# An expert stage whose token rows arrive in 256-byte runs and are turned by VectorE, with all first matrices resident in SBUF

## What is computed

```python
h = layernorm(x)
logits = h @ Wg + bg                                  # 8 experts
vals, idx = top_k(logits, 2); w = softmax(vals)       # each token goes to 2 experts
hid = relu(h @ W1[e] + b1[e])                         # W1: 8 x 256 x 512
eo  = hid @ W2[e] + b2[e]                             # W2: 8 x 512 x 256
mixed = sum(eo[idx] * w)
x = x + layernorm_affine(mixed + h, gamma, beta)
```

## Time and profile before

| | us |
|---|---|
| median of 3 runs | 2424.22 (2422.47 to 2425.36) |
| span of the profiled execution, from its first to its last instruction | 2425.2 |

### The profile page before, as it was taken

One profiled execution on the slowest core, in us unless ns is written; L12 is line 12 of the kernel. 1 busy time (PEld: TensorE's weight loads), 2 busy tenths in 40 slices (PEclk: granted clock), 3 DMA queues, 4 the chain that ended last, 5 costly groups with the idle time before them and its releaser, 6 DMA issues. The chain is left out here.

```text
span 2425.2 us, 47399 instructions
## 1 busy us (share of the span) xinstructions
PE 2186.3 (90%) x13721; PEld 1766.3 (73%) x13722; DVE 2038.4 (84%) x3037; ACT 1506.5 (62%) x3292; POOL 1827.8 (75%) x1093
## 2 busy tenths in 40 slices
PE   8889899998989898998989898999787999999980
PEld 5667677677777666777777776767676999999970
DVE  5999999999999999999999999999974555555558
ACT  6687877878786877878787878877741111111106
POOL 3888989889898989889888989898962434444447
PEclk9999999999999999999999999999987999999995
DMA  5041322314041323324041413223137998999978
GB/s 172 7 134 54 131 75 102 124 52 164 21 158 48 131 69 114 106 70 153 32 156 34 144 49 135 80 96 116 62 123 199 226 228 229 229 230 229 229 166 277
DMA packets 186791, 312.50 MB, mean 129 GB/s; under 512 B 18851, under 2 KB 118083, under 8 KB 186500
## 3 DMA queue, kind: packets, MB, share of 16 engines
q1 hardware_dynamic: 140932, 258.53, 33.4%
q0 software_dynamic: 25584, 34.62, 7.5%
q10 hardware_dynamic: 20112, 17.32, 2.2%
HBM read 247.09 MB, written 63.32 MB: 128 GB/s over the span
## 5 line engine op out<-in xcount | busy, mean ns | idle before, releaser
L855 POOL TENSOR_TENSOR dbu<-drive_u,b_rows 128x1024 f32<-128x1024 f32 x384 | 904.3, 2363 | 87.7 <-DVE ps_a L660 35.1
L1159 ACT ACTIVATE ps_a<-delta,a_neg 128x512 f32<-128x512 f32 x768 | 517.2, 685 | 136.9 <-DVE ss L660 120.2
L872 POOL TENSOR_TENSOR wp<-ss,rows_c 128x1024 f32<-128x1024 f32 x192 | 453.6, 2363 | 37.6 <-DVE ss L660 36.9
L1766 POOL DMA_INDIRECT acc_scratch<-ow,idx x135 | 211.2, 1564 | 309.2 <-issue 102.4
L672 DVE TENSOR_TENSOR wd<-ps_a,rows_c 128x1024 f32<-128x1024 f32 x320 | 383.3, 1198 | 0.0
L1437 PEld LDWEIGHTS ps_y<-ident,wd 128*128 128x128 f32 x2560 | 299.4, 143 | 98.7 <-issue 70.5
L1437 PE MATMUL ps_y<-ident,wd 128*128 128x128 f32 x2560 | 337.3, 277 | 12.4 <-DVE wd L672 12.4
L1804 ACT COPY e_meta<-xt 128x2 f32<-128x2 f32 x135 | 25.9, 192 | 439.0 <-PE e_ps_x L1877 294.4
L1464 PEld LDWEIGHTS ps_a<-dg,duT 128*128 128x128 f32 x2048 | 248.6, 196 | 60.6 <-issue 58.1
L1464 PE MATMUL ps_a<-dg,duT 128*128 128x128 f32 x2048 | 259.0, 281 | 31.6 <-ACT carry L1166 28.6
L1688 DVE TENSOR_SCALAR e_hT<-e_ps_h,b_turned 128x128 f32<-128x128 f32 x540 | 152.1, 344 | 144.7 <-PE e_ps_h L1886 125.2
(11 more groups left out here) (200 smaller groups left out, 3653.8 us busy)
## 6 DMA issues: line engine op xcount, KB each, us to landing
b_rows<-in_L_ffn_W_dram SPq DMA_DIRECT2D x135, 512.0 KB
rows_c<-b_scratch SPq DMA_DIRECT2D x128, 512.0 KB, 4.9
b_rows<-b_scratch SPq DMA_DIRECT2D x96, 512.0 KB, 4.1
xt<-xs_scratch SPq DMA_DIRECT2D x135, 129.0 KB
xb<-in_L_attn_x_dram SPq DMA_DIRECT2D x16, 512.0 KB, 4.0
hx<-in_L_attn_x_dram SPq DMA_DIRECT2D x16, 512.0 KB, 6.3
x_scratch<-hx SPq DMA_DIRECT2D x16, 512.0 KB, 2.9
acc_scratch<-stage SPq DMA_DIRECT2D x16, 512.0 KB, 2.9
```

The source lines that it names most:

```text
L855: pool.tensor_tensor(dbu[:, k % NBU], du[:, g % 2, :].unsqueeze(1).broadcast_to([P, 2, CH]), bb[:, row:row + 2, :], ALU.mult).then_inc(dbu ...
L872: pool.tensor_tensor(wp[:, s % 2], ss[:, s % 2], cc[:, rows, :], ALU.mult).then_inc(wp_done, 1)
L1159: act.activation(dst, dl[:, g, :], ACT.Exp, scale=a_neg[:, g, n:n + 1]).then_inc(exp_done, 1)
L1766: pool.indirect_dma_start(out=acc_dram, out_offset=bass.IndirectOffsetOnAxis(ap=idx[:, old, :], axis=0), in_=ow[:, old, :], in_offset=None ...
```

## The change

The rows of a tile now load with four DMAs, one for each quarter of the 256 columns, each into 32 partitions. Partition 32 i + b of a slot holds, for each j of 4, columns 64 i to 64 i + 63 of row 32 j + b: 128 runs of 256 bytes in each DMA. A fifth DMA loads weight and row number of 128 rows, 8 bytes each, into `xm`. VectorE turns the slot in one instruction of 32x32 blocks into `xT`, in which partition p then has columns 2p and 2p + 1. TensorE no longer turns anything, and `e_ps_x` is only kept as space for the last stage (`e_ps_n`). W1 is stored in the matching order, rows 2p and 2p + 1 in partition p.

All 8 first matrices (4 MB) stay in SBUF, in `w1_all`, one tensor that holds the Mamba block's `win` and `b_rows` before. Seven DMAs load them while the last chunk ends. Per tile there is no W1 load and no second value load on SyncE; ScalarE copies the tile's W1 (128x1024) inside SBUF to one of two buffers `w1s` instead.

```diff
+            sync.wait_ge(proj_full, full("z", 3, NC - 1))
+            sync.dma_start(*w1_parts[0]).then_inc(w1_in, 16)
             for h in range(2):
+                for m in ((0, 1, 3, 4), (6, 7))[h]:
+                    sync.wait_ge(dbu_done, products(t, m))
+                    sync.dma_start(*w1_parts[brow(m) + 1]).then_inc(w1_in, 16)
                 sync.wait_ge(wd_done, ND * t + (3, 5)[h])
                 sync.wait_ge(wp_done, 3 * t + (2, 3)[h])
                 sync.dma_start(*experts[h]).then_inc(w_ready, 16)
...
-            sync.wait_ge(tabs, 11)
-            for j in range(W1_EARLY):
-                e = sync.value_load(tabi[0:1, 1, j:j + 1], min_val=0, max_val=E - 1)
-                sync.dma_start(w1[:, j], w1_t[:, bass.ds(e, 1)].rearrange("p e k f -> p (e k) f")
-                               ).then_inc(w1_in[j], 16)
...
-                wait_apart(sync, passed, [(x_copied, 1, t, 1 - RING)])
-                sync.dma_start(xt[:, slot, :], xs_dram[bass.ds(off, P), :]).then_inc(t_in[slot], 16)
-
-            def load_weights(t, slot):
-                e = sync.value_load(tabi[0:1, 1, bass.ds(t, 1)], min_val=0, max_val=E - 1)
-                wait_apart(sync, passed, [(h_full, 1, t, 1 - RING)])
-                sync.dma_start(w1[:, slot], w1_t[:, bass.ds(e, 1)].rearrange("p e k f -> p (e k) f")
-                               ).then_inc(w1_in[slot], 16)
+                wait_apart(sync, passed, [(x_turned, 1, t, 1 - RING), (meta_copied, 1, t, 1 - RING)])
+                rows = xs_dram[bass.ds(off, P), :].rearrange("(j b) d -> b j d", b=BLK)
+                for i in range(QB):
+                    sync.dma_start(xt[i * BLK:(i + 1) * BLK, slot], rows[:, :, i * D // QB:(i + 1) * D // QB]
+                                   ).then_inc(t_in[slot], 16)
+                with nc.allow_non_contiguous_dma(reason="a weight and a row number for each row"):
+                    sync.dma_start(xm[:, slot], xs_dram[bass.ds(off, P), D:]).then_inc(t_in[slot], 16)
...
+                if real(s):
+                    wait_slot(dve, t_in[slot], s, RING, slot, per=16 * PARTS)
+                    wait(dve, h_full, 1, s, -1)
+                    dve.transpose(xT[:, par], xt[:, slot].rearrange("p j (a k) -> p j k a", k=KD)).then_inc(x_turned, 1)
                 if real(s - 1):
...
+            act.wait_ge(tabs, 11)
+            act.wait_ge(w1_in, 16 * (E - 1))
...
                 if real(s):
-                    wait(act, x_turned, 1, s, 1)
+                    e = act.value_load(tabi[0:1, 1, bass.ds(s, 1)], min_val=0, max_val=E - 1)
+                    wait(act, h_full, 1, s, -1)
+                    act.copy(w1s[:, par].rearrange("p k f -> p (k f)"), w1[:, bass.ds(e * (KD * F), KD * F)]
+                             ).then_inc(w1_set, 1)
+                    wait_slot(act, t_in[slot], s, RING, slot, per=16 * PARTS)
                     wait(act, o_weighed, 1, s, 1 - RING)
-                    act.copy(meta[:, slot, :], xt[:, slot, D:])
-                    wait(act, h_full, 1, s, -1)
-                    act.copy(xT[:, par].rearrange("p k n -> p (k n)"), ps_x[:, par, 0:KD * P]).then_inc(x_copied, 1)
+                    act.copy(meta[:, slot, :], xm[:, slot]).then_inc(meta_copied, 1)
...
-                if real(s):
-                    wait_slot(pe, t_in[slot], s, RING, slot)
-                    wait(pe, x_copied, 1, s, -1)
-                    for k in range(KD):
-                        ins = pe.transpose(ps_x[:, par, k * P:(k + 1) * P], xt[:, slot, k * P:(k + 1) * P], ident[:])
-                    ins.then_inc(x_turned, 1)
                 if real(s - 1):
                     t = s - 1
-                    wait(pe, x_copied, 1, t, 1)
-                    wait_slot(pe, w1_in[(slot + 3) % RING], t, RING, (slot + 3) % RING)
+                    wait(pe, x_turned, 1, t, 1)
+                    wait(pe, w1_set, 1, t, 1)
                     wait(pe, h_done, 1, t, -1)
                     for j in range(KF):
                         for k in range(KD):
-                            ins = pe.matmul(ps_h[:, 1 - par, j, :], w1[:, (slot + 3) % RING, k, j * P:(j + 1) * P],
-                                            xT[:, 1 - par, k, :], start=(k == 0), stop=(k == KD - 1))
+                            ins = pe.matmul(ps_h[:, 1 - par, j, :], w1s[:, 1 - par, k, j * P:(j + 1) * P],
+                                            xT[:, 1 - par, :, k, :], start=(k == 0), stop=(k == KD - 1))
```

More of the change, by code:

```diff
@@ L16 @@
 U32 = mybir.dt.uint32
-W1_RING = 4
-W1_EARLY = 1
+RING = 4
+BLK = 32
 def wait(eng, sem, per, c, k):
@@ L83, in mamba_moe_kernel @@
                             W2[half].rearrange("e (k p) d -> p e k d", p=P)))
-        b_rows = ctx.enter_context(nc.sbuf_tensor("b_rows", [P, (N - 4) * CH], F32))
+        w1_all = ctx.enter_context(nc.sbuf_tensor("w1_all", [P, KD * 2 * DI + (N - 4) * CH], F32))
+        win_flat = w1_all[:, 0:KD * 2 * DI]
+        b_rows = w1_all[:, KD * 2 * DI:]
         delta = ctx.enter_context(nc.sbuf_tensor("delta", [P, G * CH], F32))
         drive_u = ctx.enter_context(nc.sbuf_tensor("drive_u", [P, 2 * CH], F32))
-        assert E * D == G * CH and W1_RING * KD * F <= (N - 4) * CH
-        w1 = b_rows[:, 0:W1_RING * KD * F].rearrange("p (r k f) -> p r k f", r=W1_RING, k=KD)
-        w1_t = W1.rearrange("e (k p) f -> p e k f", p=P)
+        assert E * D == G * CH and E * KD * F == KD * 2 * DI + (N - 4) * CH and 2 * KD * F == KD * 2 * DI
+        w1_t = W1.rearrange("e (p k) f -> p e (k f)", k=KD)
+        w1_e = w1_all[:].rearrange("p (e n) -> p e n", e=E)
+        w1_parts = [(w1_e[:, 0:2], w1_t[:, 0:2])] + [(w1_e[:, e], w1_t[:, e]) for e in range(2, E)]
         b2b, gm, bt = delta[:], drive_u[:, 0:D], drive_u[:, D:2 * D]
@@ L93, in mamba_moe_kernel @@
         small_in = ctx.enter_context(nc.semaphore("rows_loaded"))
-        w1_in = [ctx.enter_context(nc.semaphore(f"w1_loaded{i}")) for i in range(W1_RING)]
+        w1_in = ctx.enter_context(nc.semaphore("w1_loaded"))
         expert_rows = ((b1r, b1.rearrange("e (k p) -> (e k) p", p=P), b1_in),
@@ L100, in mamba_moe_kernel @@
                     W_out, Wg, bg, xs_dram, ident, turned_h, tabi, aside, tabs, aside_done, scat, order, order_done, acc_dram, rows_c, experts, w_in,
[L101 removed]
+                    win_flat, b_rows, delta, drive_u, expert_rows, w1_parts, w1_in, NC, D, DI, G, KD, N, R, TAPS, HALO)
         moe_block(nc, x1_dram, out.rearrange("b l d -> (b l) d").rearrange("(c i p) d -> c p i d", p=P, i=NT),
                   xs_dram, ident, tabi, aside, tabs, aside_done, scat, order, order_done, acc_dram,
[L104 removed]
+                  w1_all, w1_in, w2, w_in, b1r, b1_in, b2b, gm, bt, small_in, NC, D, KD, E, F)
 def xs_region(tiles):
@@ L113, in mamba_block @@
                 W_out, Wg, bg, xs_dram, ident, turned_h, tabi, aside, tabs, aside_done, scat, order, order_done, acc_dram, rows_c, experts, w_ready,
-                b_rows, delta, drive_u, expert_rows, w1, w1_t, w1_in, NC, D, DI, G, KD, N, R,
+                win_flat, b_rows, delta, drive_u, expert_rows, w1_parts, w1_in, NC, D, DI, G, KD, N, R,
                 TAPS, HALO):
@@ L143, in sem @@
             return ctx.enter_context(nc.semaphore(name))
-        win = sb("win", [P, KD, 2 * DI])
+        win = win_flat.rearrange("p (k n) -> p k n", k=KD)
         wxp = sb("wxp", [P, G, R + 2 * N])
@@ L1529, in moe_block @@
 def moe_block(nc, x1_dram, out_t, xs_dram, ident, tabi, aside, tabs, aside_done, scat, order, order_done, acc_dram,
-              w1, w1_t, w1_in, w2, w_in, b1r, b1_in, b2b, gm, bt, small_in, NC, D, KD, E, F):
+              w1, w1_in, w2, w_in, b1r, b1_in, b2b, gm, bt, small_in, NC, D, KD, E, F):
     KF = F // P
@@ L1536, in moe_block @@
     LAG = 2
-    RING = W1_RING
+    QB = P // BLK
+    PARTS = QB + 1
     PEEL = LAG + 5 + (NTT - LAG - 5) % RING
@@ L1565, in moe_block @@
         nb = sb("r_nb", [P, SLOTS, CT])
-        xt = sb("xt", [P, RING, XW])
+        xt = sb("xt", [P, RING, QB, D // QB])
+        xm = sb("xm", [P, RING, 2])
         meta = sb("e_meta", [P, RING, 2])
         idx = sb("idx", [P, RING, 1], U32)
-        xT = sb("xT", [P, 2, KD, P])
+        xT = sb("xT", [P, 2, QB, KD, BLK])
+        w1s = ee[:, LOADS - 2 * KD * F // W:].rearrange("p s n -> p (s n)").rearrange("p (r k f) -> p r k f", r=2, k=KD)
         hT = sb("e_hT", [P, 2, KF, P])
@@ L1573, in moe_block @@
         ow = sb("ow", [P, RING, D])
-        ps_x = ctx.enter_context(nc.psum_tensor("e_ps_x", [P, 2, CH], F32))
+        ps_n = ctx.enter_context(nc.psum_tensor("e_ps_n", [P, 2, CH], F32))
         ps_h = ctx.enter_context(nc.psum_tensor("e_ps_h", [P, 2, KF, P], F32))
@@ L1577, in moe_block @@
         ps_b = ctx.enter_context(nc.psum_tensor("e_ps_b", [P, 2, CH], F32))
-        sums = [ps[:, b] for ps in (ps_x, ps_h[:].rearrange("p b k n -> p b (k n)"), ps_o) for b in range(2)]
+        sums = [ps[:, b] for ps in (ps_n, ps_h[:].rearrange("p b k n -> p b (k n)"), ps_o) for b in range(2)]
```

(8 more changed lines are left out.)

## The result

The changed kernel takes 2396.72 us, median of 4 runs (2394.97 to 2398.82), beside 2424.79 for the kernel before (4 runs, 2422.47 to 2427.07): a ratio of 0.9885, 95% interval 0.9871 to 0.9899. It is faster by 28 us, where 4 us slower was forecast. All that was forecast to happen on SyncE's queue happened; the queue is only a little quicker than the sum had it.

What follows compares the result with a forecast made beforehand. SyncE's queue replaces TensorE as bound at 3.78 us a tile: 1846.0 + 23.7 + 480.1 + 2.7 + 2.6 = 2355.0 us to tile 134's matmuls, against 2350.87; the span grows 4.1, the median to 2428.3 us, range 2395 to 2450.

Steps and rivals of the forecast that it cites:

- first row issue: SyncE's queue, start of the expert tiles: the first row load's issue stays at 1846.00 us.
- seven peeled tiles: SyncE's queue, tiles ahead of the loop: 1.10 + 4 x 0.57 = 3.38 us each, 23.7 us in the sum.
- 127 periods: SyncE's queue, from the loop's first tile to tile 134: 3.78 us of work per tile, 480.1 us.
- the price of a further issue: SyncE's queue: each of three added DMA issues per tile costs 0.57 us, within 0.34 to 0.73.
- the value load: SyncE's queue: the value load that goes per tile is worth 0.65 us, within 0.56 to 0.84.
- break-even: SyncE's period per tile at which the change neither gains nor loses: 3.75 us.
- issues are cheap, TensorE stays the bound: Rival, expert tiles: with i below 0.48 the period is 3.52 us, the time 2396 us; chance 0.25.
- i: Price of each of the three further issues per tile on SyncE's queue, taken at 0.57 us.
- The prediction's own sign of being wrong: Expert tiles: TensorE still busy 50.00 of 50 us would show the forecast wrong.
- the early load: End of the first block: the single early matrix load goes; nothing waited for it but the first matmuls.
- TensorE's 93% in the tile stage: Expert tiles: TensorE is busy some 93% and waits for VectorE's turning, which waits for a load.
- Its sum of 3.52 a tile: VectorE, per tile: busy time, idle steps at value loads and a 0.45 us turning make 3.52 us, under SyncE's 3.78.

Runs made afterwards that it cites:

- six_issues: The changed kernel with the 8-byte pieces of each tile loaded a second time on SyncE, into a buffer nothing reads: 2469.99 us.
- small_sixth: The changed kernel with one more issue per tile on SyncE, a single run of 8 bytes: 2475.39 us.
- xm_on_act: The changed kernel with the load of the 8-byte pieces moved from SyncE's to ScalarE's queue: 2392.08 us, ratio 0.9870 to the kernel before.
- two_turns: The changed kernel in which VectorE turns every slot twice, the first time into a buffer that nothing reads: 2396.03 us.

## Why the prediction was wrong

The sum of the prediction against the trace of the changed kernel:

| term | forecast, us | measured, us | difference |
|---|---|---|---|
| first row issue | 1846.00 | 1842.56 | -3.4 |
| seven peeled tiles | 23.7 | 23.5 | -0.2 |
| 127 periods | 480.1 (3.78 each) | 450.4 (3.546 each) | -29.7 |
| tile 134: issues, landing, turning | 5.3 | 6.0 | +0.8 |
| from its first matmul to the end | 74.3 | 74.6 | +0.3 |

Together -32.2 (the differences are of the unrounded terms), from the forecast span of 2429.3 to 2397.1.

- **The step that failed is the price of a further issue**, taken at 0.57, above the 0.54 of the earlier trace rows, "because each issue has an address to work out". It is 0.51 with its address. 3 x 0.06 is 0.18 of the 0.234 us per period; the value load, 0.71 where 0.65 was taken, gives 0.06 more. At 127 periods a tenth of a microsecond is 13 us, and here it decided the sign: break-even was 3.75. The lone issue of 0.34 in the earlier trace rows had spoken for a price below that of the rows in which issues stand behind each other into full DMA engines.
- **The mechanism was right.** SyncE's queue took TensorE's place, its wait vanished, and a sixth issue costs its full price. The rival "issues are cheap, TensorE stays the bound" named nearly the time, 2396, and not the way: its condition, i below 0.48, is not met, and one issue fewer still gains 4.6 us. With i = 0.51 alone the prediction's own sum gives 3.60 a tile and about 2403 us; the value load at 0.71 and the earlier start make the rest, less what other terms give back. The prediction's own sign of being wrong, TensorE at 50.00 of 50, came although its mechanism held: SyncE's period is only 0.04 us longer than TensorE's.
- The Trainium skill's rule (page "DMA: Bandwidth & Descriptors", section "Issuing engines are not separate DMA queues") says that the time for initiating a DMA is usually small beside the DMA itself. In this kernel it sets the pace all the same: six_issues and small_sixth pay 0.53 and 0.58 us per tile for 1 KB and for 8 bytes.
- **"The first row issue stays at 1846.00" failed too**, by 3.4 us: 1.9 (4.55 - 2.67) are the early load, of which the prediction said only that nothing waited for it, and 1.5 stand ahead of the last scatter, where executions differ by more.
- The seven peeled tiles came out right by luck. Most stand 3.1 to 3.2 us apart, where 3.38 was forecast, but the row loads of the fourth took 2.86 us in place of 1.82, and the step into the loop is longer. Why the fourth was held stays open.
- TensorE's 93% in the tile stage was wrong with the period: it is over 99%. Its own period of 3.52 was right (3.51 in the chain of xm_on_act).
- VectorE: 0.45 for the turning was right (0.44). Its sum of 3.52 a tile was not its limit, as two_turns shows, for the idle steps in it give way. The estimate of 0.62 from the Trainium skill's figure for bf16 (page "VectorE: DVE Perf Modes", section "The three transpose paths") was too high.
- ScalarE's copy, 1.04 forecast, takes 1.05, and TensorE never waits for it in the list of waits. The DMA share, forecast at 0.4 to 0.85, is 0.58 to 0.60. The matrix loads at the end of block 1 show no delay that others wait for: the issue behind the routing counts stands at 1829.42 and, in the other runs with these loads, at 1822.68 to 1829.85, without them at 1829.20 and 1830.97.

## What to carry to other kernels

Count the DMA instructions per tile on each issuing queue as you would count matmuls: here each costs 0.51 us with its address for 32 KB, a sixth one 0.53 for 1 KB and 0.58 for 8 bytes, and a value load 0.71. Before such a sum decides a sign, ask how far its least known price stands from the break-even; where one hundredth of a microsecond per tile is 1.3 us, a price that a few rows of the trace give only to within a tenth is a question and not an answer. And when an engine reads 50.00 of 50, look at the chain and at the waits of the queues before calling it the only bound: two periods 1% apart look alike in a busy share.

## What the hardware showed that was not expected

- Joining issues can slow a queue: row loads whose read pattern has an outermost step of 4 or 2 had at most 8 or 4 packets under way, and the issues behind them are held (1.73 and 2.35 us in the rows above, in place of 0.35), while a load of 512 runs with an outermost step of 128 takes 0.39 us and holds nothing.
- A value load on VectorE runs for the most part beside an instruction of 0.44 us that was put ahead of it (idle steps 40.2 us without, 11.8 with it); on SyncE an added one lengthens the period by 0.71 us.
- One 512 KB load whose data nobody awaits at that point delayed the end of a block by about 2 us (4.55 us from the last scatter's end with it, 2.46 without).
